# RWKV mixing and gated FFN on eight cores: x tiles 4 to 7 in GpSimd's queue, chunk 1's first gate units in parts, identity products in the prologue

## The reference

```
xn  = (x - mean) / sqrt(var + 1e-5)
k, r = xn @ Wk.T, xn @ Wr.T ; v = r
y   = wkv_scan(-exp(time_decay), time_first, k, v)     # recurrence over tokens, per channel
att = (sigmoid(r) * y) @ Wo.T
ffn = (silu(xn @ Wg.T / 127) * (xn @ Wu.T / 127)) @ Wd.T / 127     # int weights, 3072 hidden
out = x + att + ffn
```

## Time and profile before

| | us |
|---|---|
| median of 3 runs | 1359.73 (1359.24 to 1359.89) |
| the profiled execution | 1359.52 |
| its span on the slowest core (core 3) | 1358.0 |
| spans of the eight cores | 1355.6 to 1358.0 |
| TensorE busy (matmuls) | 1334.7 |
| VectorE, ScalarE, GpSimd busy | 674.6, 396.5, 35.2 |

### The profile page before, as it was taken

How to read it: one execution, slowest core, us unless ns; L and a number is a source line. 1 busy time by engine, 2 the same in 40 slices (tenths; PEclk the granted TensorE clock), 3 DMA queues, 4 the chain that set the end, 5 groups by cost and what they waited for, 6 DMA issues and landing times.

```text
span 1358.0 us, 17854 instructions; the slowest of 8 cores (1355.6 to 1358.0 us)
## 1 busy us (share of the span) xinstructions
PE 1334.7 (98%) x6208; PEld 606.6 (45%) x6208; DVE 674.6 (50%) x1101; ACT 396.5 (29%) x663; POOL 35.2 (3%) x70
## 2 busy tenths in 40 slices
PE   4999999999999999999999999999999999999999
PEld 2444444444444444444444444444444444444444
DVE  4666666515952288323873238721487215672211
ACT  5554545312331233212332123221233212221100
POOL 0111111000000000000000000000000000000000
PEclk9999999999999999999999999999999999999999
DMA  9699989953554544545545444544455443334411
GB/s 231 144 183 196 209 163 181 204 142 120 167 144 148 168 137 135 147 150 176 125 117 163 155 156 124 143 152 156 150 143 126 155 155 124 94 102 164 153 47 55
DMA packets 90376, 200.41 MB, mean 148 GB/s; under 512 B 32816, under 2 KB 35888, under 8 KB 90160
## 3 DMA queue, kind: packets, MB, share of 16 engines
q1 hardware_dynamic: 55584, 167.81, 39.0%
q0 software_dynamic: 9360, 25.17, 12.5%
q10 hardware_dynamic: 25344, 6.29, 2.5%
HBM read 184.56 MB, written 33.55 MB: 161 GB/s over the span
## 4 chain that ended last, share of the span: by engine, by line
PE 98%; DMA 2%; SPq 0%; issue 0%; DVE 0%; DVEq 0%; POOLq 0%
PE ps L309 33%; PE ps L313 33%; PE ps_o L327 24%; PE ps_o L334 8%; DMA ring<-w_gu 1%; DMA x_buf<-x_tm 1%; PE ps L291 0%; SPq L170 0%; DVE xres L556 0%; DVEq L555 0%; POOLq L255 0%
## 5 line engine op out<-in xcount | busy, mean ns | idle before, releaser
L309 PE MATMUL ps<-xn,ring 128*128 128x512 bf16 x2048 | 485.5, 380 | 4.1 <-DMA ring<-w_gu 3.9
L313 PE MATMUL ps<-xn,ring 128*128 128x512 bf16 x2048 | 484.7, 379 | 0.0
L549 DVE SCALAR_TENSOR_TENSOR h_act<-ps,silu 128x512 bf16<-128x512 f32 x192 | 132.5, 690 | 438.4 <-PE ps L313 427.5
L327 PE MATMUL ps_o<-wd_bf,h_act 128*128 128x512 bf16 x1536 | 342.0, 379 | 0.0
L309 PEld LDWEIGHTS ps<-xn,ring 128*128 128x128 bf16 x2048 | 200.5, 98 | 246.1 <-issue 6.2
L313 PEld LDWEIGHTS ps<-xn,ring 128*128 128x128 bf16 x2048 | 200.7, 98 | 242.6 <-issue 1.7
L420 ACT ACTIVATE silu<-ps 128x512 f32<-128x512 f32 x192 | 114.6, 597 | 452.7 <-PE ps L309 452.4
L327 PEld LDWEIGHTS ps_o<-wd_bf,h_act 128*128 128x128 bf16 x1536 | 150.3, 98 | 181.3
L334 PE MATMUL ps_o<-wo_bf,outp 128*128 128x512 bf16 x512 | 120.9, 379 | 0.0
L402 ACT ACTIVATE den<-den 128x512 f32<-128x512 f32 x64 | 40.3, 630 | 260.1 <-DVE den L537 259.9
L556 DVE TENSOR_TENSOR xres<-xres,ps_o 128x512 f32<-128x512 f32 x64 | 44.0, 688 | 87.0 <-PE ps_o L334 86.4
(11 more groups left out here) (40 smaller groups left out, 319.1 us busy)
## 6 DMA issues: line engine op xcount, KB each, us to landing
ring<-gu_bfd SPq DMA_DIRECT2D x144, 512.0 KB, 3.3
ring<-kr_bfd SPq DMA_DIRECT2D x48, 512.0 KB, 3.9
xres<-x_tm SPq DMA_DIRECT2D x64, 256.0 KB, 5.5
out_tm<-xres SPq DMA_DIRECT2D x64, 256.0 KB, 4.7
x_buf<-x_tm SPq DMA_DIRECT2D x28, 512.0 KB, 6.4
ring<-w_gu POOLq DMA_DIRECT2D x24, 512.0 KB, 11.3
gu_bfd<-ring SPq DMA_DIRECT2D x24, 512.0 KB, 7.4
ring<-w_kr POOLq DMA_DIRECT2D x8, 512.0 KB, 7.4
```

Of the source, the lines that this page charges most:

```text
L309: ins = te.matmul(bank(kind, idx, 0), w[:, gc * D:(gc + 1) * D], xn[c % 2][:, gc, :], start=(gc == 0), stop=(gc == G - 1))
L313: ins = te.matmul(bank(kind, idx, 1), w[:, C + gc * D:C + (gc + 1) * D], xn[c % 2][:, gc, :], start=(gc == 0), stop=(gc == G - 1))
L327: te.matmul(ps_o[i % 2], h_act[c % 2][:, hg * TC + tt * D:hg * TC + (tt + 1) * D], wd_bf[:, half, hg * 512:(hg + 1) * 512], start=(hg == 0 ...
L549: ve.scalar_tensor_tensor(out=h_act[c % 2][:, hg * TC:(hg + 1) * TC], in0=bank("gu", i, 1), scalar=1.0 / (127.0 * 127.0), in1=silu[i % 3], ...
```

## The change

- SyncE asks for x tiles 0 to 3 only. GpSimd waits for tile 2 (not 3), and its queue is then: weight tile 0, 1, x tiles 4, 5, weight tile 2, 3, x tiles 6, 7, weight tile 4 (with its waits), ...
- td and tf are asked for by ScalarE; its first activation is now exp(td). The three residual tiles are asked for after weight tile 8. The write-back of tiles 0 to 2 waits until tile 3 has landed.
- Transposes have banks of their own (`tr_bank`: `ps_o`, for tiles 1 and 3 the third pair), and no slots. Each half waits for its own half's copy (`evacuated`).
- TensorE multiplies the identity by itself 100 times after the identity is there, and 16 times after each of the transposes 0 to 3 (`keep_running`), into a bank that gate unit 0 overwrites.
- Gate units 3, 4, 5 are done in parts of tokens 0 to 255, 256 to 383 and 384 to 511 (`gu_part`): units 3 and 4's first parts, transposes 6, unit 5's first part, transposes 7, the second parts of the three, the third parts of the three. Kr 0 stands ahead of them, kr 1 behind.
- The orders of VectorE and ScalarE follow: the steps of one x tile run one after another, tiles 6 and 7 behind kr 0's maximum and exponentials; `att_scan` is divided into `att_z` (up to zA) and the scans.

The core of the diff; like moves on ScalarE and VectorE are cut:

```diff
-SLOTS = [("tr", l0) for l0 in range(NT)]
-SLOTS += [("gu", 0), ("tr", 4), ("gu", 1), ("tr", 5), ("gu", 2), ("tr", 6), ("tr", 7), ("kr", 0)]
+SLOTS = [("gu", 0), ("gu", 1), ("gu", 2), ("kr", 0)]
...
+        def tr_bank(l, k):
+            return pair[2][k] if l in (1, 3) else ps_o[k]
...
-                for l in range(2 * NX):
+                for l in range(NX):
                     x_load(l)
-                sy.dma_start(out=tdt, in_=td_hbm).then_inc(sem["io_td"], 16)
-                sy.dma_start(out=tft, in_=tf_hbm).then_inc(sem["io_tf"], 16)
-                for i in range(3):
-                    res_load(i)
...
-                            sy.wait_ge(*loaded(n))
+                            sy.wait_ge(*loaded(max(n, R - 1)))
                             sy.dma_start(out=scr[row], in_=ring[n % R]).then_inc(sem[f"wb{n % R}"], 16)
+                            if n == 8:
+                                for i in range(3):
+                                    res_load(i)
...
-                gp.wait_ge(sem["xl3"], 16)
+                def x_second(l):
+                    gp.dma_start(out=x_tile(l),
+                                 in_=x_hbm[l * D:(l + 1) * D, :]).then_inc(x_landed(l)[0], 16)
+
                 for n in range(NS):
+                    if n == 0:
+                        gp.wait_ge(*x_landed(2))
+                    if n == 2:
+                        x_second(4)
+                        x_second(5)
+                    if n == 4:
+                        x_second(6)
+                        x_second(7)
...
+                def evacuated(l, k):
+                    te.wait_ge(sem["v_ev" if k else "s_ev"], l + 1)
 
                 def tr(l):
-                    acquire("tr", l)
                     te.wait_ge(sem["s_xt"], l + 1)
                     for cb in range(G):
-                        ins = te.matmul(bank("tr", l, cb // 4)[:, (cb % 4) * D:(cb % 4 + 1) * D],
+                        if l >= 2 and cb % 4 == 0:
+                            evacuated(l - 2 if l < 5 else l - 1, cb // 4)
+                        ins = te.matmul(tr_bank(l, cb // 4)[:, (cb % 4) * D:(cb % 4 + 1) * D],
                                         xt[l % 2][:, cb * D:(cb + 1) * D], ident, start=True, stop=True)
                     ins.then_inc(sem["t_tr"], 1)
...
+                def gu_part(i, t0, t1):
+                    c = GU[i][0]
+                    if t0 == 0:
+                        acquire("gu", i)
+                        te.wait_ge(*loaded(RING_AT[("gu", i)]))
+                    w = ring[RING_AT[("gu", i)] % R]
+                    for m in range(2):
+                        for gc in range(G):
+                            if m == 0 and gc % 4 == 0:
+                                evacuated(NT * c + t1 - 1, gc // 4)
+                            ins = te.matmul(bank("gu", i, m)[:, t0 * D:t1 * D],
+                                            w[:, m * C + gc * D:m * C + (gc + 1) * D],
+                                            xn[c][:, gc, t0 * D:t1 * D],
+                                            start=(gc == 0), stop=(gc == G - 1))
+                        if t1 == NT:
+                            ins.then_inc(sem["t_u" if m else "t_g"], 1)
...
+                def keep_running(n):
+                    for _ in range(n):
+                        te.matmul(pair[0][0][:, 0:D], ident, ident, start=True, stop=True)
+
                 te.wait_ge(sem["g_id"], 1)
+                keep_running(100)
                 for l in range(NT):
                     tr(l)
+                    keep_running(16)
                 xn_ready(0)
                 proj("gu", 0, 0, "t_g", "t_u")
                 tr(4)
                 proj("gu", 1, 0, "t_g", "t_u")
                 tr(5)
                 proj("gu", 2, 0, "t_g", "t_u")
+                proj("kr", 0, 0, "t_k", "t_r")
+                gu_part(3, 0, 2)
+                gu_part(4, 0, 2)
                 tr(6)
+                gu_part(5, 0, 2)
                 tr(7)
-                proj("kr", 0, 0, "t_k", "t_r")
-                xn_ready(1)
-                for s in range(1, 2 * G):
+                for t in range(2, NT):
+                    for i in range(3, 6):
+                        gu_part(i, t, t + 1)
+                proj("kr", 1, 1, "t_k", "t_r")
+                for s in range(2, 2 * G):
...
 (ScalarE)
+                sc.dma_start(out=tdt, in_=td_hbm).then_inc(sem["io_td"], 16)
+                sc.dma_start(out=tft, in_=tf_hbm).then_inc(sem["io_tf"], 16)
                 sc.wait_ge(sem["v_c"], 1)
+                sc.wait_ge(sem["io_td"], 16)
+                sc.activation(out=etd, in_=tdt, func=Act.Exp).then_inc(sem["s_etd"], 1)
                 ln_rstd(0)
+                ln_xt(0)
                 ln_rstd(1)
-                ln_xt(0)
+                ln_xt(1)
...
+                gate(2)
+                att_exp(0)
+                ln_rstd(6)
+                ln_rstd(7)
+                ln_xt(6)
                 ln_xt(7)
-                gate(2)
                 ln_ev(6)
                 ln_ev(7)
-                att_exp(0)
-                for s in range(1, 2 * G):
+                for i in range(3, 6):
+                    gate(i)
+                att_rec(0)
+                att_exp(1)
...
 (VectorE)
                 ffn_h(2)
+                att_max(0)
+                ln_bn(6)
+                ln_bn(7)
+                ln_nb(6)
+                ln_nb(7)
+                att_z(0)
                 ln_ev(6)
+                ve.wait_ge(sem["s_ew"], 1)
+                att_scan(0)
                 ln_ev(7)
-                att_max(0)
-                for s in range(1, 2 * G):
+                att_den(0)
+                for i in range(3, 6):
+                    ffn_h(i)
+                att_max(1)
+                att_out(0)
...
```

## The result

| | before | changed |
|---|---|---|
| median | 1359.81 us (1359.24 to 1359.94) | 1368.35 us (1366.74 to 1370.86) |
| ratio | | 1.0065 (95% interval 1.0048 to 1.0083) |
| span of the slowest core, profiled execution | 1358.0 | 1366.5 (core 5) |
| fastest core of it | 1355.6 | 1354.2 (core 0) |

The account below looks back on a forecast made before the run. Gapless TensorE matmuls bound the kernel after 24 us; 3.3 + 2.5 us won were lost to waits, bank and parts (2.95 + 1.3 + 0.5 + 0.3) and unit 3's later end; kr 2 1.5 later gave 1361.0, range 1355.8 to 1365.0.

Parts of the forecast that it names:

- unit 1's clock: Gate unit 1, behind transposes 4: full clock, 3.45 us a unit, with no slow-clock cost in the sum.
- the time from tile 4's issue to tile 6's landing: Weight ring ahead of kr 2: 18.0 us, from 16.9 to 19.3, landing tile 6 at 68.05.
- the clock behind kr 2: Kr 2 starts at 68.05, 1.5 us later than before, with no slow-clock cost added.
- Start of the first unit: First gate unit: layer norm sets its start, moved from 23.94 to 20.6 us (21.9 if the table load stays).
- Unit 0 at full clock: Gate unit 0: identity products keep the clock up, so it costs 3.45 instead of 5.96 us, saving 2.5.
- x4's statistics: Layer norm of x tile 4: x4 lands at 23.3, so transposes 4 run at 27.0 after a 2.95 us wait.
- the parts: Gate units 3 to 5 in parts: 3.55 us a unit against 3.45, 0.3 in all.
- the small wait named: Unit 6: a small wait of TensorE for a DMA, starting at 56.4 as tile 4 lands at 56.35.
- the first rival: Prologue: x4 is no obstacle and the ring is quick; kr 2 at 63.5, 1356.4 us; chance 0.25.
- late x4 and clock: Transposes 4: x4 lands at 25.6, 5.2 us idle, unit 1 may cost 2.5 more; 1364.5 us; chance 0.33.
- first bytes at 13.3: GpSimd's first weight row: issued at some 10.4, first bytes between 12.6 and 14.6 us, taken as 13.3.
- cost nothing: Small loads of td and tf from ScalarE's queue: no cost.

Follow-up runs that it names:

- the spaced run: Changed kernel with GpSimd's queue reordered (tile 0, x4, tile 1, x5, tiles 2, 3, x6, x7), tile 6 asked for only after kr 1's first half: 1364.8 us, ratio 1.0041.
- the held write-backs: Changed kernel with GpSimd's queue reordered and started after x tile 1, write-backs of tiles 4 and 5 held until tile 6 landed: 1360.7 us, ratio 1.0007.
- the two runs on the kernel before: Kernel before with weights after x tile 2, identity products, down-weight blocks four tiles later: 1365.6 us; the same plus td and tf asked for by ScalarE: 1359.1.
- the new order alone: Changed kernel with GpSimd waiting for x tile 1, then tile 0, x4, tile 1, x5, tiles 2, 3, x6, x7: 1364.2 us, ratio 1.0036.
- down-weight blocks later: Changed kernel with the down-weight blocks asked for four ring tiles later, behind tiles 8 to 31 instead of 4 to 27: 1366.9 us, ratio 1.0048.
- x in SyncE's queue: Changed kernel with x tiles 4 to 7 back in SyncE's queue behind tiles 0 to 3: 1366.5 and 1367.0 us, ratio 1.005.
- unit 3 first: Changed kernel with the last two parts of units 3, 4, 5 done unit by unit, tile 7's copy ahead of the first scans: 1366.9 us, ratio 1.0049.

## Why the prediction was wrong

**The places of the waits were right, the size was not:** 1.5 us forecast, 8.5 measured. The sign came out, but the prediction had not vouched for it: it called differences under 2.7 us undecidable and gave "slower" a chance of 0.33. What failed are three terms: unit 1's clock, put at nothing in the sum; the time from tile 4's issue to tile 6's landing, taken as 18.0; and the clock behind kr 2, put at nothing. By the prediction's own steps, on core 5:

- Start of the first unit: 20.6 forecast, 21.52 (18.7 to 22.1 over the cores). Unit 0 at full clock: yes. The products ended at 9.36 (forecast 9.6).
- x4's statistics at 24.12 (23.3), transposes 4 at 28.27 (27.0), a wait of 3.13 (2.95). Right within 1.3 us.
- **Unit 1's clock, the first failed step.** I gave a slow clock to a rival that began at a wait of 5.2 us. A wait near the forecast one was enough: 5.14 instead of 3.45 us here, and a slow unit 1 on all six cores that waited 2.90 us or more. Kr 0 ends at 41.2 instead of 38.25.
- Transposes 6 waited 0.91 (1.3), kr 1 0.86 (0.5), the parts were as priced. Tile 4 was asked for at 52.77 (50.05), unit 6 began at 59.82 (56.4) with the small wait named.
- **Tile 6, the second failed step.** I took 18.0 us from tile 4's issue "a little under the middle" of 16.9 to 19.3, because it would be asked for sooner. It took 20.5. The issue is no help (the spaced run), and the earlier trace rows had shown core 3's 19.3 beside a share of 1.00. The writes beside it are worth some 3 us (the held write-backs), the down-weight blocks also some 3 (15.7 to 16.3 instead of 17.8 to 20.5 us on the slow cores). The last 1.2 us, from 19.3 to 20.5, are in two numbers: from 2.5 us after tile 4's issue to tile 6's landing core 5 wrote 3.15 MB at 176 GB/s, core 3 of the kernel before 3.02 MB at 180. Why more was written ahead of it was not found.
- **The clock behind kr 2, the third.** The wait was forecast in kind; that it costs 1.7 us more was not counted. Only core 5 paid this; it makes it the slowest, 2.0 us behind core 7.

The terms add up: unit 3 ends 2.7 us later than forecast (1.3 at transposes 4, 1.7 of clock, 0.4 less at transposes 6, 0.1 elsewhere), tile 6's 2.5 and the last clock's 1.7 make 6.9 of the 7.0 us between 1361.0 and core 5's 1366.5 with 1.5 around it.

Behind the last two stands, as I read it, one choice: each unknown was taken near its middle, while the metric takes the worst of eight cores of which four are slow at once. Cores 0 and 2 were what the first rival says (core 0: x4 at 19.9, tile 4 in 5.2, kr 2 at 62.75), and the metric does not see them. The rival "late x4 and clock" had the right mechanism, and its 52.4 for tile 4's issue is close to the 52.77 measured, at 1364.5 with a third of the chance. Part of that is luck: it was to hold from x4 landing after 24.5 us, with 5.2 us of wait and 2.5 more in unit 1. On core 5 x4 was there at 24.12, the wait was 3.13 and unit 1 cost 1.7 more.

**A part that the sum left without a price:** the DMA's idle stretch from 10 to 14 us, which the sum contained (first bytes at 13.3). At the 259 GB/s of the earlier trace rows it is an estimated 0.9 MB that the slow cores lacked. That the moved loads of td and tf "cost nothing" held, but they are what makes an earlier start possible at all (the two runs on the kernel before). By the Trainium skill (TensorE: Matmul & The Clock Gate, What's actually happening) idleness closes the gate again; the clock column agrees, with 0.50 behind the wait of 3.13 us.

## What to carry to other kernels

Where a ring's first reload is 0.6 us from binding on a full DMA, as here, a faster start is easily lost: first take bytes from that place (write-backs, loads due later), or let the tile's last reader end sooner, and only then start earlier. Price a wait of TensorE of 3 us with the slow clock behind it, count the wait that a faster unit ahead of it adds, and sum for the core that comes off worst, not for a typical one. When loads move from one queue to another, look what fills the DMA in the gap, and what small loads stand behind the big ones.

## What the runs showed of the hardware

- In the changed kernel's profile the DMA of one core of each neighbouring pair moved less, and which one was slow changed from execution to execution: tile 6 took 14.4 to 15.1 us from tile 4's issue on one and 17.8 to 20.5 on the other. From 2.5 us after that issue to the landing core 0 wrote 231 GB/s and core 5 176, both with a share above 1.00. The split is not in every profile: before, tile 6 took 16.9 to 19.6 us, and with the new order alone both cores 6 and 7 were late (19.0 and 20.1). The cause was not tried.
- Behind the first unit, TensorE ran on at full clock after every wait of 2.0 us or less. Waits of 2.0 to 3.0 us went either way: full clock after 2.65, 2.88 and two of 3.0, half clock after 2.08 (down-weight blocks later, core 7), 2.40 (x in SyncE's queue, core 3) and 2.49 (unit 3 first, core 4). After all waits of 3.02 to 5.7 us it ran at half for most of the next unit, and the clock column shows 0.50 then. What decides between them was not found.
- GpSimd's queue took some 2.8 us to its first bytes on an empty DMA (asked for at 11.26, share 0.03 from 12 to 14), as the 2.2 of the earlier trace rows had half shown. Next to nothing else moved in that time.
